# Top layer of a recommender tower: dense rows on four row groups, and VectorE folds the last column block

## The reference

```python
def _cin_layer(x0, xi, W):
    F0_, Fi, Fn = (x0.shape[1], xi.shape[1], W.shape[-1])
    Wr = W.reshape(F0_, Fi, Fn)
    return jnp.einsum('bid,bjd,ijn->bnd', x0, xi, Wr)
h = x
outs = []
for W in (W0, W1, W2):
    h = _cin_layer(x, h, W)
    outs.append(h)
res = jnp.concatenate(outs, axis=1)
z = jnp.sum(res, axis=-1)
...
h = jnp.concatenate([z, dense_ctx], axis=1)
h = jnp.maximum(h @ W_top1 + b_top1, 0.0)
h = jnp.maximum(h @ W_top2 + b_top2, 0.0)
y = h @ W_top3
```

## Time and profile before

| what | value |
|---|---|
| median of 3 runs | 1166.59 us (1166.09 to 1166.8) |
| the profiled execution's own time | 1167.73 us |
| its span in the trace | 1165.9 us |
| PE busy | 1125.9 us (97%) |
| DVE, ACT, POOL busy | 879.1, 562.2, 763.6 us |

### The profile page before, as it was taken

How to read it: one execution, slowest core, us unless ns; L and a number is a source line. 1 busy time by engine, 2 the same in 40 slices (tenths; PEclk the granted TensorE clock), 3 DMA queues, 4 the chain that set the end, 5 groups by cost and what they waited for, 6 DMA issues and landing times.

```text
span 1165.9 us, 20547 instructions
## 1 busy us (share of the span) xinstructions
PE 1125.9 (97%) x4682; PEld 797.4 (68%) x4682; DVE 879.1 (75%) x2757; ACT 562.2 (48%) x1815; POOL 763.6 (65%) x660
## 2 busy tenths in 40 slices
PE   3899999999999999999999999999999999999999
PEld 2676666766677666667667666666667776667765
DVE  2787878887865778888786587888786588878830
ACT  3244545455543455455553355545554354555631
POOL 6686868768683675868685485877768268545630
PEclk9899999999999999999999999999999999999989
DMA  7574443331436224243442434233243621513000
GB/s 265 126 196 95 100 92 76 62 93 35 111 89 163 60 38 103 58 91 81 92 112 62 111 82 92 76 80 74 37 117 80 163 74 31 122 60 120 1 1 1
DMA packets 127789, 102.69 MB, mean 88 GB/s; under 512 B 77457, under 2 KB 86865, under 8 KB 127026
## 3 DMA queue, kind: packets, MB, share of 16 engines
q1 hardware_dynamic: 117522, 92.79, 32.0%
q0 software_dynamic: 8192, 2.11, 2.0%
q10 hardware_dynamic: 1952, 6.40, 1.4%
HBM read 97.06 MB, written 4.20 MB: 87 GB/s over the span
## 4 chain that ended last, share of the span: by engine, by line
PE 86%; DVE 5%; issue 4%; DMA 2%; POOL 2%; ACT 0%; DVEq 0%; SPq 0%; POOLq 0%; ACTq 0%
PE tps L789 19%; PE acc L747 19%; PE tps L791 18%; PE tps L790 18%; PE side L816 5%; DVE parts_sb L546 3%; PE side L803 2%; PE acc L743 1%; PE side L811 1%; PE tps L881 1%; POOL rows_sb L470 1%; DVE z_sb L516 1%; DMA roll_sb<-x_halves 1%; PE side L763 1%; DVE parts_sb L542 0%
## 5 line engine op out<-in xcount | busy, mean ns | idle before, releaser
L546 DVE SCALAR_TENSOR_TENSOR parts_sb<-tps,xcol_sb,parts_sb 128x128 f32<-128x128 f32 x2432 | 671.8, 343 | 194.1 <-PE tps L791 187.6
L634 ACT ACTIVATE y_sb<-tps,xcol_sb 128x128 f32<-128x128 f32 x1536 | 439.6, 370 | 526.9 <-PE tps L791 526.8
L789 PE MATMUL tps<-w_hi_sb,h_hi_sb 128*128 128x512 f32 x1024 | 511.7, 500 | 13.0 <-DVE parts_sb L546 9.7
L790 PE MATMUL tps<-w_lo_sb,h_hi_sb 128*128 128x512 f32 x1024 | 404.6, 395 | 0.0
L791 PE MATMUL tps<-w_hi_sb,h_lo_sb 128*128 128x512 f32 x1024 | 404.3, 395 | 0.0
L789 PEld LDWEIGHTS tps<-w_hi_sb,h_hi_sb 128*128 128x128 f32 x1024 | 192.4, 188 | 131.5 <-issue 46.4
L408 POOL DMA_INDIRECT rows_sb<-tables,rows_now_sb x240 | 230.4, 960 | 71.6 <-issue 43.7
L747 PE MATMUL acc<-prod_sb,w_sb 128*128 128x512 f32 (+1 forms) x544 | 269.4, 584 | 4.6 <-DVE prod_sb L499 4.5
L423 POOL TENSOR_TENSOR ysum_sb<-y_sb 128x1024 f32<-128x1024 f32 x64 | 153.8, 2403 | 172.5 <-ACT y_sb L634 171.8
L790 PEld LDWEIGHTS tps<-w_lo_sb,h_hi_sb 128*128 128x128 f32 x1024 | 192.8, 188 | 87.7 <-issue 57.3
L791 PEld LDWEIGHTS tps<-w_hi_sb,h_lo_sb 128*128 128x128 f32 x1024 | 192.3, 188 | 46.9
(11 more groups left out here) (56 smaller groups left out, 366.7 us busy)
## 6 DMA issues: line engine op xcount, KB each, us to landing
roll_sb<-x_scratch SPq DMA_DIRECT2D x240, 256.0 KB
w_sb<-w_rows SPq DMA_DIRECT2D x40, 256.0 KB, 3.5
gsum_sb<-w_rows ACTq DMA_DIRECT2D x8, 512.0 KB, 9.1
roll_sb<-x_halves SPq DMA_DIRECT2D x32, 128.0 KB, 3.0
rows_sb<-tables,rows_now_sb POOLq DMA_INDIRECT x240
x_scratch<-rows_sb SPq DMA_DIRECT2D x30, 128.0 KB, 3.9
xx_sb<-x_scratch SPq DMA_DIRECT2D x15, 256.0 KB, 2.7
roll_sb<-x_scratch SPq DMA_DIRECT2D x30, 64.0 KB
```

The lines of the kernel that those rows point to most:

```text
L546: dve.scalar_tensor_tensor(part, bank, scale, part, ALU.mult, ALU.add).then_inc(d_done, 1)
L634: done = act.activation(y[:, pair % Y_RING, half * CH + u * NF:half * CH + (u + 1) * NF], tps[:, p % RING, u * NF:(u + 1) * NF], ACT.Copy, ...
L789: pe.matmul(bank, h1_hi[:, par, cols], w1_hi[:, of], start=True, stop=False, skip_group_check=True)
L790: pe.matmul(bank, h1_hi[:, par, cols], w1_lo[:, of], start=False, stop=False, skip_group_check=True)
```

## The change

- `dense` and the 16 last rows of `W_top1` are loaded four times, copy m to partitions 32m to 32m + 15, and of the weights only the 128 columns of m. `add_part(m, 3)` takes copy m, so the four matmuls read from four different groups of rows. Thirteen loads raise `top_loaded` where seven did.
- For the last column block of the last chunk POOL stops after L427. The two halvings, the sum with `parts` and the write of `h2t` are done by DVE behind its last bank, chained by a new semaphore `last_step`.

```diff
@@ -183,7 +183,8 @@
         top = roll[:].rearrange("p r a n -> p (r a n)")
         wt1 = top[:, 0:4 * HIDDEN1].rearrange("p (k n) -> p k n", k=4)
         wt2 = top[:, 2048:2048 + 4 * HIDDEN2].rearrange("p (k n) -> p k n", k=4)
-        dense = top[0:DENSE, 3072:3072 + BATCH]
+        dense = [top[32 * m:32 * m + DENSE, 3072:3072 + BATCH] for m in range(4)]
+        wt1_dense = [wt1[32 * m:32 * m + DENSE, 3, 0:P] for m in range(4)]
         wt3 = top[:, 3584:3584 + 2]
         bt1 = top[:, 3592:3596]
         bt2 = top[:, 3600:3602]
@@ -240,6 +241,7 @@
         d_done = sem("d_done")
         a_done = sem("a_done")
         y_step = sem("y_step")
+        last_step = sem("last_step")
         h2t_ready = sem("h2t_ready")
         xdiag_ready = sem("xdiag_ready")
         g_filled = sem("g_filled")
@@ -384,10 +386,10 @@
                         sp.dma_start(w2_end[:], ins["w2_rows"][:, end_at:FIELDS, :]).then_inc(w2_end_loaded, 16)
                         for dst, src in (
                             (wt1[:, 0:3, :], ins["W_top1"][0:3 * P, :].rearrange("(k p) n -> p k n", p=P)),
-                            (wt1[0:DENSE, 3, :], ins["W_top1"][3 * P:3 * P + DENSE, :]),
+                            *((wt1_dense[m], ins["W_top1"][3 * P:3 * P + DENSE, m * P:(m + 1) * P]) for m in range(4)),
                             (wt2, ins["W_top2"].rearrange("(k p) n -> p k n", p=P)),
                             (wt3, ins["w_top3_cols"]), (bt1, ins["b_top1_cols"]),
-                            (bt2, ins["b_top2_cols"]), (dense, ins["dense_rows"]),
+                            (bt2, ins["b_top2_cols"]), *((rows_in, ins["dense_rows"]) for rows_in in dense),
                         ):
                             sp.dma_start(dst, src).then_inc(top_loaded, 16)
 
@@ -425,7 +427,7 @@
                     pool.wait_ge(a_done, t * N_A + 2 * (pair + 1))
                     pool.wait_ge(y_step, before + at // 2 - 1)
                     pool.tensor_tensor(ysum[:], ysum[:], y[:, pair % Y_RING], ALU.add).then_inc(y_step, 1)
-                if at == 2 * PAIRS - 1:
+                if at == 2 * PAIRS - 1 and not (is_last(t) and s == SUB - 1):
                     pool.wait_ge(y_step, before + PAIRS - 1)
                     pool.tensor_tensor(ysum[:, 0:CH], ysum[:, 0:CH], ysum[:, CH:2 * CH], ALU.add).then_inc(y_step, 1)
                     pool.wait_ge(y_step, before + PAIRS)
@@ -474,7 +476,6 @@
             pool.wait_ge(ids_loaded, 32)
             gather(1, 1, slice(0, STEPS), gathered[1])
             each_chunk(pool, chunk)
-            finish_block(PER_BLOCK - 2, CHUNKS - 1, SUB - 1)
 
         @block.vector
         def _(dve):
@@ -581,6 +582,18 @@
                         take_bank(q, t, p)
 
             each_chunk(dve, chunk)
+
+            last = SUB - 1
+            dve.wait_ge(y_step, ((CHUNKS - 1) * SUB + last) * STEPS_OF_SUM + PAIRS - 1)
+            dve.tensor_tensor(ysum[:, 0:CH], ysum[:, 0:CH], ysum[:, CH:2 * CH], ALU.add).then_inc(last_step, 1)
+            dve.wait_ge(last_step, 1)
+            dve.tensor_tensor(ysum[:, 0:CH // 2], ysum[:, 0:CH // 2], ysum[:, CH // 2:CH], ALU.add).then_inc(last_step, 1)
+            dve.wait_ge(last_step, 2)
+            dve.wait_ge(d_done, CHUNKS * QUAD * N_D)
+            dve.tensor_tensor(ysum[:, 0:CH // 2], ysum[:, 0:CH // 2], parts[:, last % 2].rearrange("p u n -> p (u n)"),
+                              ALU.add).then_inc(last_step, 1)
+            dve.wait_ge(last_step, 3)
+            dve.tensor_tensor(h2t[:, (CHUNKS - 1) % 2, last, :], ysum[:, 0:NF], ysum[:, NF:2 * NF], ALU.add).then_inc(h2t_ready, 1)
 
         @block.scalar
         def _(act):
@@ -717,7 +730,7 @@
                 copy_g(PER_BLOCK - 1, CHUNKS - 1, use)
             copy_z2(CHUNKS - 1)
             copy_z3(BLOCKS - 1)
-            act.wait_ge(top_loaded, 16 * 7)
+            act.wait_ge(top_loaded, 16 * 13)
             for m in range(4):
                 act.wait_ge(hid_done, m + 1)
                 act.activation(hid1[:, m, :], tps[:, m, :], ACT.Relu, bias=bt1[:, m:m + 1]).then_inc(hid_copied, 1)
@@ -877,12 +890,14 @@
             each_chunk(pe, chunk)
 
             def add_part(m, part):
-                rows_in = slice(0, DENSE if part == 3 else P)
-                return pe.matmul(tps[:, m, :], wt1[rows_in, part, m * P:(m + 1) * P], dense if part == 3 else z[:, part, :],
+                if part == 3:
+
+                    return pe.matmul(tps[:, m, :], wt1_dense[m], dense[m], start=False, stop=False, skip_group_check=True)
+                return pe.matmul(tps[:, m, :], wt1[:, part, m * P:(m + 1) * P], z[:, part, :],
                                  start=part == 0, stop=part == 2, skip_group_check=True)
 
             form_g(PER_BLOCK - 1, CHUNKS - 1, 0)
-            pe.wait_ge(top_loaded, 16 * 7)
+            pe.wait_ge(top_loaded, 16 * 13)
             pe.wait_ge(z1_summed, CHUNKS)
             pe.wait_ge(d_done, CHUNKS * QUAD * N_D)
             pe.wait_ge(a_done, CHUNKS * N_A)
```

## The result

Nine runs of each: 1162.76 us median with the change (1160.05 to 1164.79), 1166.8 us before (1166.01 to 1169.19). The ratio is 0.9963, 95% interval 0.9954 to 0.9972: faster by 0.37%, 4.04 us between the medians. The profiled execution of the changed kernel took 1164.79 us, the slowest of its nine, with a span of 1162.9 us.

The account below looks back on a forecast made before the run. TensorE was taken to bound the kernel. Earlier short matmuls (3.35 us) plus full clock (3.83) minus remaining low clock (1.70) gave 5.48 us less; the median was put between 1161.1 and 1162.25, at 1161.6 us, range 1159.4 to 1165.0.

Parts of the forecast that it names:

- VectorE's fold: Program's end: VectorE instead of POOL folds the last block in 2.2 us, so the second `form_g` starts 0.56 us earlier.
- The dense rows: Dense matmuls behind `form_g`: four row groups together take 0.86 us instead of 4.88, hidden under ACT's copy, costing nothing.
- What ends the wait: Before the short L811 matmuls: ACT's copy releases them, at 1125.09 instead of 1128.44, 3.35 us earlier.
- The clock: End of the program: low clock for 3.4 us instead of 10.24; 3.83 us gained at full clock, 1.70 paid back.
- the sum: Profiled span: 3.35 + 3.83 - 1.70 = 5.48 us less, ending at 1160.44 instead of 1165.92.
- two readings of the 1.14 us: Median 1.14 us below the profiled execution: profiler's effect (1161.1 us) or less low-clock time in those runs (1162.25 us).
- The rule on gaps: TensorE's clock: the skill says gaps between bursts lower it, short ones do not; the trace of the kernel before disagrees.
- A longer low time: Rival, 20%: at the end the clock stays low for 6.8 or 10.2 us; 1162.8 to 1164.5 us.
- No fall: Rival, 17%: the clock doesn't fall at the end; gain 7.18 us, 1159.4 us.
- Serial row groups: Rival, 10%: the dense matmuls' four row groups do not run together; gain 1.5 to 2.4 us, 1164.2 to 1165.1 us.
- The slower case: Rival, 3%: the new gap before L811 keeps the clock down; with 21 us low, 1169.9 us for the median.
- The loads: Six more loads, 3.6 us on SP, cost nothing; PE needs them at 1118.4, with cover of nearly 50 us.

Follow-up runs that it names:

- One part alone: Only the fold on VectorE, dense rows on one row group as before; against the kernel before: 1166.6 us (11 runs), ratio 0.9991.

## Why the prediction was right, and where its size was off

- **VectorE's fold.** Priced at 2.2 us after POOL's last sum; it took 1.96 (1121.22 to 1123.18), for its parts at 0.69, 0.42, 0.42 and 0.29 the nearest rows had given 0.68, 0.41, 0.41 and 0.34. The gain was put at 0.56 us and was 0.46: `form_g` starts 5.44 and not 5.34 us after the first one, because 0.52 and not 0.43 us pass from the last 128-row record to the first 64-row one. One part alone gave the 0.44 again, and 0.5 us in the medians.
- **The dense rows.** Right at the cheap end: two rounds, 1.14 us with the latency, all under ACT's copy. Predicted start of the short matmuls: 8.49 us after the first `form_g`; measured: 8.56.
- **What ends the wait.** Right: ACT's copy.
- **The clock.** For the profiled execution the term was right, 3.4 us of low clock instead of 10.24. That execution's tail became 5.3 us shorter, where the sum had 5.48. That the low time was 3.4 us there is in part luck: another execution of the same kernel had none. The step that was off is the one from there to the median. "37.48 us, of which 7.66 at half speed" took the low time of one execution for that of the kernel. It was the longest of three (10.2, 6.8, 3.4), and the changed kernel's is not a constant 3.4 us either. Mean against mean the low time gives 2.3 us, not the 3.4 that 10.24 against 3.4 makes. That is 1.1 us of the difference between 5.0 us forecast and 4.04 measured. Another 0.3 us is in the order of events: without its clock terms the sum had 2.06 us (5.48 less 3.42), and the tails at full clock differ by 1.8. Of the two readings of the 1.14 us between profile and median, less time at the low clock fits better (the profiled execution had the longest low time of three), but no run separates them. What the prediction did not consider is that the end's start alone spreads over 2.8 us between executions.
- **The rule on gaps.** The prediction held the rule of the Trainium skill (TensorE: Matmul & The Clock Gate, "Why this matters for your kernels") against the trace. For this end the runs bear the trace out: from the second `form_g` to the fall the kernel before has no gap, and its clock fell in all three executions; with 128 rows in the same matmuls it did not in the one profiled. The changed kernel, which has a gap of 0.92 us, was without a fall in one of three. That gaps matter too is not excluded: near 390 us the clock fell behind a wait of 1.76 us and 128-row matmuls, though in the profile of the kernel before it did not fall there behind one of 2.26 us.
- **The rivals.** A longer low time did not occur in three executions. No fall, given 17%, did in one of the three; it is no rival but the other face of the same kernel. Serial row groups are excluded by the 1.14 us. The slower case never showed: the low time shrank in the mean.
- **The loads.** Nothing waited for the six more; TensorE's wait in front of the z matmuls is still released by VectorE's last bank, 0.70 us as before.

## What to carry to other kernels

When a profile shows a stretch at the low clock, look what TensorE did ahead of it, and not only whether it was busy: here 3.4 us of matmuls on 16 rows were followed by low clock that cost 1.7 to 5.1 us. Take the low time from several executions before it goes into a sum, and compare ends from a fixed event, so that the spread of what comes before does not hide a gain of a few tenths of a percent. When a change opens a gap, ask whether what waits can be released earlier; here moving one matmul behind it was worth most of a microsecond more.

## What was not expected of the hardware

Eight 16-row records on four row groups start in two rounds and end within 1.14 us, where the same records on one group took 3.70 us at full clock; that is the four-fold of which only the two-fold was to be seen before. The low time at the end was 0, 3.4, 6.8 or 10.2 us, differing between executions of one and the same program, and every microsecond of it cost the end half a microsecond. And a busy TensorE did not keep its clock: with 16 rows in 3.7 us of matmuls it fell in all three executions, with 128 rows in matmuls of the same length it did not in the one profiled, and the whole-span clocks of five runs say the same.
